# The second attention's softmax: sixteen ACT exponentials per tile that read the scores in place and give the denominators

## What is computed

```python
sim = jnp.einsum('bhid,bjd->bhij', q, k)          # 16 heads x 77 keys per token
attn = jax.nn.softmax(sim, axis=-1)
out = jnp.einsum('bhij,bjd->bhid', attn, v)
out = out.transpose(0, 2, 1, 3).reshape(b, n, INNER) @ Wo
ff = xn @ Wff1
h, gate = (ff[..., :FF_INNER], ff[..., FF_INNER:])
out = out + jax.nn.silu(gate) * h @ Wff2
```

## Time and profile before

| | |
|---|---|
| median of the runs | 526.7 us |
| profiled execution | 527.4 us (span of the core 525.3) |
| granted clock of PE, mean over the span | 0.951 |
| busy: PE, DVE, POOL, ACT | 89%, 71%, 58%, 44% of the span |
| second attention, by the timeline | about 262 to 421 us |

### The profile page before, as it was taken

One profiled execution on the slowest core, in us unless ns is written; L12 is line 12 of the kernel. 1 busy time (PEld: TensorE's weight loads), 2 busy tenths in 40 slices (PEclk: granted clock), 3 DMA queues, 4 the chain that ended last, 5 costly groups with the idle time before them and its releaser, 6 DMA issues.

```text
span 525.3 us, 11394 instructions
## 1 busy us (share of the span) xinstructions
PE 465.8 (89%) x3381; PEld 398.3 (76%) x3381; DVE 374.6 (71%) x1237; ACT 229.3 (44%) x558; POOL 305.8 (58%) x377
## 2 busy tenths in 40 slices
PE   6668999999999699999878999999999689999950
PEld 5446799899987557776647888889898589999940
DVE  4874799999984323333468899999999556676727
ACT  2453666666653445555423434343524124444410
POOL 6336459889854227777334467676776624576640
PEclk9778999999999979999998999999999979999985
DMA  8999970000004723321110011110000013222016
GB/s 216 354 346 348 362 278 17 21 22 22 21 21 145 263 67 93 89 65 40 48 30 21 11 30 32 31 31 12 21 12 21 22 49 85 66 77 63 30 49 209
DMA packets 42930, 49.16 MB, mean 94 GB/s; under 512 B 7809, under 2 KB 28636, under 8 KB 42871
## 3 DMA queue, kind: packets, MB, share of 16 engines
q1 hardware_dynamic: 36991, 39.57, 24.2%
q0 software_dynamic: 4544, 8.44, 4.9%
q10 hardware_dynamic: 1336, 0.43, 0.5%
HBM read 20.97 MB, written 28.35 MB: 94 GB/s over the span
## 4 chain that ended last, share of the span: by engine, by line
PE 75%; DVE 13%; POOL 4%; issue 2%; DMA 2%; ACT 2%; SPq 0%; POOLq 0%; DVEq 0%; ACTq 0%
PE ps L1620 10%; PE ps L1473 7%; PE ps L1603 7%; PE ps L1609 6%; PE ps L1566 6%; PE ps L1544 5%; PE ps L1521 3%; PE ps L1385 3%; PE ps L1296 3%; PE ps L1558 2%; PE ps L1568 2%; PE ps L1595 2%; PE ps L1629 2%; PE ps L1388 2%; PE ps L1453 1%
## 5 line engine op out<-in xcount | busy, mean ns | idle before, releaser
L561 POOL DMA_INDIRECT ys<-ysbs,backs x78 | 76.9, 986 | 53.9 <-issue 20.9
L506 POOL TENSOR_TENSOR qr<-qsm,mhalf 128x16 f32<-128x16 f32 x16 | 47.3, 2957 | 20.2 <-DVE qsm L882 20.1
L1237 DVE TENSOR_TENSOR big<-big,ps 128x256 f32<-128x256 f32 x39 | 16.4, 422 | 50.4 <-ACT big L747 50.4
L499 POOL DMA_INDIRECT rows<-pays,slots x32 | 33.2, 1038 | 20.5 <-DVE slots L1011 11.5
L527 POOL DMA_INDIRECT rows<-pays,slots x32 | 32.7, 1023 | 19.7 <-DVE slots L1085 14.4
L518 POOL TENSOR_TENSOR pp<-pp,rden 128x1232 f32<-128x1232 f32 x16 | 36.0, 2252 | 13.4 <-DVE x L1063 10.2
L752 ACT ACTIVATE big<-big 128x512 f32<-128x512 f32 x39 | 24.6, 632 | 43.2 <-PE ps L1620 36.9
L1603 PE MATMUL ps<-region_b,xsT 128*128 x78 | 42.2, 624 | 0.0
L1609 PE MATMUL ps<-xsT,wups 128*128 128x128 f32 x312 | 41.3, 275 | 0.0
L1620 PE MATMUL ps<-w2b,big 128*128 x312 | 41.1, 275 | 0.0
L1242 DVE TENSOR_TENSOR big<-ps,b1T 128x512 f32<-128x512 f32 x39 | 27.0, 692 | 18.5 <-PE ps L1609 18.0
(11 more groups left out here) (278 smaller groups left out, 1252.3 us busy)
## 6 DMA issues: line engine op xcount, KB each, us to landing
rows<-empty SPq DMA_DIRECT2D x68, 258.0 KB, 4.5
xs<-rows SPq DMA_DIRECT2D x78, 64.5 KB, 1.9
region_b<-in_L_ffn_W_dram SPq DMA_DIRECT2D x2, 1024.0 KB, 9.6
region_a<-in_L_ffn_W_dram SPq DMA_DIRECT2D x1, 2048.0 KB, 14.7
yb_all<-ys SPq DMA_DIRECT2D x16, 128.0 KB, 2.0
keys<-ys SPq DMA_DIRECT2D x8, 256.0 KB, 4.6
ys<-ysbs,backs POOLq DMA_INDIRECT x78
rows<-pays,slots POOLq DMA_INDIRECT x64, 2.5
```

The source lines that it names most:

```text
L499: pool.indirect_dma_start(rows[0][:, :], bass.IndirectOffsetOnAxis(slot[t % PB][:, k:k + 1], 0), pay[t % PB][:, k, :], None, bounds_check= ...
L506: pool.tensor_tensor(qr[s], qsm[s], mhalf[:, 0:H], ALU.pow).then_inc(a["qr"], 1)
L561: pool.indirect_dma_start(ys[l][:, :], bass.IndirectOffsetOnAxis(backs[:, j % XB:j % XB + 1], 0), ysb[j % YB], None, bounds_check=2 * T - ...
```

## The change

The keys get the opposite sign (`kT1`), so that the banks hold the negated scores; DVE takes each head's minimum of them, which is minus the maximum of the scores, with instructions of the same shapes. ACT then computes exp(-1 x S + mx), one instruction per head (77 columns, `exp_heads`), since the bias operand is one number per partition: it reads the scores in PSUM, writes `prob`, and its second output, the sum along the head, goes to `den`. The two subtractions and the sum on DVE are gone. The heads of the first bank stand in ACT's queue ahead of x2T and xT (semaphore "sub"), the other ten behind tanh (semaphore "exp"), where the one exponential stood. PE waits for "sub" of the tile before ahead of bank 0, and for "exp" of the tile before ahead of banks 1 and 2.

```diff
@@ kT1, in the prologue
-            act.activation(kT1[:, :], TP[0][:, 0:NBATCH * KEYS], ACT.Copy, scale=float(HD1) ** -0.5).then_inc(pro["kT1"], 1)
+            act.activation(kT1[:, :], TP[0][:, 0:NBATCH * KEYS], ACT.Copy, scale=-float(HD1) ** -0.5).then_inc(pro["kT1"], 1)
@@ ACT, new helper, and step1
+            def exp_heads(t, h0, h1):
+
+                s = t % 2
+                for h in range(h0, h1):
+                    ins = act.activation(prob[s][:, h * KEYS:(h + 1) * KEYS], S[h // HB][:, h % HB * KEYS:(h % HB + 1) * KEYS], ACT.Exp,
+                                         bias=mx[s][:, h:h + 1], scale=-1.0, accum_out=den[s][:, h:h + 1])
+                return ins
+
...
                     act.copy(probT[s][:, 0:4 * P], TP[0]).then_inc(a["PT0"], 1)
+                t = i - 5
+                if 0 <= t < NT:
+                    act.wait_ge(a["mx"], a.count("mx", t + 1))
+                    exp_heads(t, 0, HB).then_inc(a["sub"], 1)
                 t = i - 8
...
                 t = i - 5
                 if 0 <= t < NT:
-                    s = t % 2
-                    act.wait_ge(a["sub"], a.count("sub", t + 1))
-                    act.activation(prob[s][:, 0:HK], prob[s][:, 0:HK], ACT.Exp).then_inc(a["exp"], 1)
+                    exp_heads(t, HB, H).then_inc(a["exp"], 1)
@@ DVE, step1
                     dve.wait_ge(a["exp"], a.count("exp", t + 1))
-                    dve.reduce_sum(den[s], prob[s][:, 0:HK].rearrange("p (h k) -> p h k", h=H), AX).then_inc(a["den"], 1)
-                    dve.wait_ge(a["den"], a.count("den", t + 1))
                     dve.reciprocal(rden[s], den[s]).then_inc(a["rden"], 1)
...
-                    dve.reduce_max(mx[s][:, 0:2 * HB].rearrange("p (b h) -> p b h", b=2), S01, AX)
-                    dve.reduce_max(mx[s][:, 2 * HB:H], S2, AX).then_inc(a["mx"], 1)
+                    dve.tensor_reduce(mx[s][:, 0:2 * HB].rearrange("p (b h) -> p b h", b=2), S01, AX, ALU.min)
+                    dve.tensor_reduce(mx[s][:, 2 * HB:H], S2, AX, ALU.min).then_inc(a["mx"], 1)
...
-                t = i - 2
-                if 0 <= t < NT:
-                    s = t % 2
-
-                    dve.wait_ge(a["mx"], a.count("mx", t + 1))
-                    dve.tensor_tensor(prob[s][:, 0:2 * HB * KEYS].rearrange("p (b h k) -> p b h k", b=2, h=HB), S01,
-                                      mx[s][:, 0:2 * HB].rearrange("p (b h) -> p b h", b=2).unsqueeze(3).to_broadcast([P, 2, HB, KEYS]), ALU.subtract)
-                    dve.tensor_tensor(prob[s][:, 2 * HB * KEYS:HK].rearrange("p (h k) -> p h k", k=KEYS), S2,
-                                      mx[s][:, 2 * HB:H].unsqueeze(2).to_broadcast([P, H - 2 * HB, KEYS]), ALU.subtract).then_inc(a["sub"], 1)
@@ PE, step1
-                    if t >= 1:
-                        pe.wait_ge(a["sub"], a.count("sub", t))
                     for bank, (h0, n) in enumerate(zip(BANK_AT, BANK_HEADS)):
+                        if t >= 1:
+                            freed_by = ("sub", "exp", "exp")[bank]
+                            pe.wait_ge(a[freed_by], a.count(freed_by, t))
                         ins = mm(S[bank][:, 0:n * KEYS], xT[s], keys1[:, t // TPB, h0 * KEYS:(h0 + n) * KEYS], start=True, stop=True)
```

## The result

The changed kernel takes 586.25 us in the median of 4 runs (585.88 to 587.76) against 526.74 (523.93 to 528.68): a ratio of 1.112 with a 95% interval of 1.109 to 1.116. It is slower by 59 us, and nearly all of it lies in the second attention, whose first score matmuls start at 267.09 us against 266.21. The spans of the two profiled executions are 584.3 and 525.3 us.

A forecast was written before the change was run, and what follows sets the result against it. PE bounds the kernel and would wait for ten late heads in every tile. Profiled 527.4 us plus 46 for longer periods and ends and 16 for clock falls gave 589, 588 against the median; range 578 to 602, 8 in 10 562 to 610.

The forecast's parts named there:

- tiles 1 and 2, bank 1 late by, with falls: Second attention's start: bank 1 at 278.0 in tile 1, 5.5 us late, and at 289.35 against 282.4 in tile 2.
- tiles 3 to 15, period without a fall: Steady second attention: PE's closed circle sets a period of 11.69 us against 8.82, bank 1 ending 44.5 us late.
- from bank 1 of tile 15 to the end: Last tile: ten heads wait for PE's values and transposes, then the reciprocal; another 1.6 us.
- What bounds: Steady second attention: the chain runs through PE alone, period 8.82 us; PE, not DVE, is the last to be ready.
- The price of a head: ACT, start of one head to start of the next: 0.35 us taken, between bounds of 0.21 and 0.52.
- The constant of PE's circle: PE's period apart from the ten late heads: 6.34 us from bank 1 to gate matmuls plus 1.85, 8.19 us.
- The second circle: Through scores, minima, six early heads, x2T, xT and ten late heads: 11.5 us, just hidden by PE's circle.
- The clock: PE's idle time of 2.9 us per tile brings a fall in three of four tiles, 1.4 us each, 16 us.
- The clock holds: Rival: no clock falls at PE idle times of 2.9 us per tile, 573 us; chance 0.19.
- A dear or a nearly free read-out: Rivals on ACT's head: 0.45 to 0.52 us, 592 to 618, chance 0.14; 0.21 to 0.25, 558 to 563, chance 0.12.
- DVE's relief decides: Rival: PE's circle closes within 8.82 us, heads at or below 0.06 us, DVE's 3 us go once: 524 us; chance 0.04.
- Signs forecast: Changed profile: sixteen exponentials per tile, PE idle 2 to 4 us, period 11 to 13, DVE about half, ACT over 70%.

The follow-up runs named there:

- e8: Kernel before with one maximum per token, two exponentials reading scores in place behind x2T, xT and PT2, ahead of tanh, DVE summing: 530.04 us, ratio 1.000.
- e3: Changed kernel with twelve heads ahead of x2T and xT and four behind tanh; PE waits for the twelve ahead of banks 0 and 1: 566.38 us.
- e5: Changed kernel with all sixteen heads ahead of x2T and xT in ACT's queue, none behind tanh: 591.59 us, 1.123 times the kernel before.
- e1: Changed kernel, but PE writes bank 0 of the scores three more times while it waits ahead of bank 1: 575.04 us, 1.083 times the kernel before.
- e4: Kernel before with one maximum per token, two exponentials reading scores in place ahead of x2T and xT, DVE summing: 533.34 us, ratio 1.014.
- e2: Changed kernel without the second output of the sixteen exponentials; DVE sums the heads as before: 558.26 us, 1.052 times the kernel before.
- e7: Changed kernel with one semaphore more: bank 1 freed after six late heads, bank 2 after the last four: 560.41 us, 1.063 times the kernel before.

## Why the prediction was right, and where its terms were off

The forecast was 588 us, the measured time 586.25. The mechanism is the one that was forecast, but that the number came within 2 us is luck: its own range was 578 to 602, and terms of the sum were off in both directions and nearly cancelled. The span grew by 59.0 us where the sum had 62. The starts of bank 1 in the two traces divide it as follows (the middle column is the forecast's own working):

| | forecast | measured |
|---|---|---|
| tiles 1 and 2, bank 1 late by, with falls | 7.0 + 2 x 0.75 x 1.4 = 9.1 | 290.09 - 282.4 = 7.7 |
| tiles 3 to 15, period without a fall | 13 x (11.69 - 8.80) = 37.6 | 13 x (11.45 - 8.80) = 34.4 |
| falls of the clock, tiles 3 to 15 | 13 x 0.75 x 1.4 = 13.7 | 9 falls, 14.4 |
| from bank 1 of tile 15 to the end | 1.6 | 131.0 - 128.5 = 2.5 |

- *What bounds.* PE, not DVE: right, and e8 shows it from the other side. There DVE has 2.8 us in 20 less to do and nothing is gained.
- *The price of a head.* I took 0.35 us, the middle between a head that overlaps with its read-out (0.30) and one that must drain first (0.41). It is 0.300: it overlaps. This term was too large by 0.05, 0.5 us of the period, 6.5 us in 13 tiles. The read-out as a short instruction in the stream was right, 0.094 us against the 0.09 that the earlier trace rows gave. The head alone takes 0.206, the lower bound of 0.21. By the figures of the Trainium skill (ScalarE: Activation LUTs, section What ACT_TABLE_LOAD costs) it would be 251 ns. The rows of the heads agree with its 344 ns for one such instruction (342 in the mean), but they overlap by more than its 93 ns, and the measured 206 decides.
- *The constant of PE's circle.* I had 8.19, it is 8.45, 3.4 us in 13 tiles the other way. Bank 1 to gate matmuls is 353.50 to 360.04 = 6.54, not 6.34. Half of the 0.2 is my reading: I took the start of the scores from the chain (343.24), where an instruction begins when the one before has ended, and the timeline of the kernel before has them at 343.07, with the gate matmuls at 350.29, which makes 6.44:

```profile
343.07 2.24 PE L1544 MATMUL ps<-keys,xT 128*128 128x462 f32 x6
...
350.29 1.16 PE L1521 MATMUL ps<-xT,wff 128*128 128x128 f32 x8
```

The other half comes after the idle time: the weight load of bank 1 and its first matmul start together at 353.50, where the load had gone 0.10 ahead (342.97 and 343.07). The wait for xT is as before (0.19 us against 0.17). The 1.19 and 0.50 are as in the earlier trace rows; the last head frees bank 1 0.22 us after the next instruction of ACT begins, not 0.16 after.
- *The second circle.* That a second circle runs through the early heads is shown by e3 and e5. In the changed kernel it is hidden by about 0.4 us: ACT is idle for 0.39 us between the early heads and x2T (359.36). The formula named the wrong path: in e3 it runs through the router, rsA and rsD and not through the scores, which makes it 0.7 us longer than I had worked out.
- *The clock.* I had drawn from one gap of 3.02 us that three of four gaps of 2.9 bring a fall. The gaps are 2.36 us and 9 of 13 periods had one, at 1.6 us. So the share of falls was near, 9 against 9.75, each cost 0.2 more than I had put, and all came after a shorter gap than I had assumed; e1 shows what the falls cost by themselves.
- *The rivals.* "The clock holds" was wrong by the changed kernel's clock of 0.91; what I gave for it, 573 us, is near what e1 measured (575), where the clock does hold. A dear or a nearly free read-out is excluded by the head of 0.300 us in the changed kernel's timeline. That DVE's relief decides is excluded by the result and by e8.
- *Signs forecast.* L688 sixteen times per tile with a row for the read-out, PE idle ahead of bank 1, 2 to 4 us, period 11 to 13, clock under 1.00: all there. DVE is at 48 of 100 us, as forecast; ACT is at 60, not over 70, in part since sixteen heads are 4.8 us a tile and not 5.6.

## What to carry to other kernels

Before work is moved to an idle engine, count its instructions, not its elements: 1232 columns cost 1.22 us in one instruction and 4.8 us in sixteen, and an idle share of 60% on that engine does not help if the place in its queue lies in the circle of the bound engine. When a buffer with one copy is freed by a later step than before, follow the circle from its writer through every queue back to its writer; if it is longer than every other circle, its sum is the new period. Others close through the queues without touching the buffer, as in e3 and e4. And free such a buffer piece by piece: one more semaphore was worth 26 us here, 10 by the period and most of the rest by the clock.

## What the runs showed of the hardware

- ACT's second output is an instruction of its own, ACTIVATION_READ_ACCUMULATOR, with a row of 0.19 to 0.27 us, of which 0.094 shows between the starts of two heads (0.300 us with it, 0.206 without, e2).
- Idle times of PE of 2.36 us (2.54 twice) once per 11.5 to 13.1 us came with a fall of the clock to 1.2 GHz in 9 of 13 tiles, those of 2.01 to 2.04 us in e3 in 3 of 7. After idle times of 1.45 us (e2) or of 1.14 and 0.18 us (e7), once per tile, it stayed at 1.00 from 300 to 440 us. Writing bank 0 three more times in the idle time (e1) kept it at 1.00 and made the kernel 11 to 15 us faster.
- An exponential read its input from PSUM about as fast as from SBUF: 924 columns took 1.03 us (e4), with a bias operand. From the 1.22 us of 1232 columns in SBUF, less 308 columns at the prediction's 0.86 ns and with its 0.1 us for the operand, an estimate is 1.05.
